# Two softmax tiles in flight and scores on 64x32 array tiles: one change to a fused AdaLN, attention, GRU and FFN kernel

## The chip, the cores and the metric

The kernel runs on one core of a Trainium2 chip. The metric is the device time in microseconds (us) of one execution, lower is better. Five engines matter: TensorE (PE for its matmuls, PEld for its weight loads), VectorE (DVE), ScalarE (ACT), GpSimd (POOL) and SyncE (SP), which issues all the DMAs. Each runs its own list of instructions in order and waits for the others on semaphores.

## The reference, cut to what matters

```python
# x [128, 32, 256]; cond [128, 256]; 32 heads of 8
x = x + attention(cond_adaln(x, query=cond[1]))      # part A
x = x + ffn(gru(initial_state=cond, inputs=x))       # part B

def cond_adaln(x):     # 8 block sums per sequence, softmax-weighted, projected, added; layer norm
    blk  = x.reshape(B, 8, 4, 256).sum(2)
    keys = rms_norm(blk @ Wk.T) * rms_weight
    w    = softmax(keys @ query)
    return layer_norm(x + (w @ blk) @ Wo.T) * gamma + beta

def attention(h):      # causal, with a linear position bias
    q, k, v = split(h @ W_attn + b_attn)
    s = q @ k.T / sqrt(8)                            # per head, 32 x 32
    p = softmax(where(causal, s, -10000) + bias)
    return (p @ v) @ W_proj + b_proj

def gru(h, xs):        # 32 sequential steps on [128, 256]
    r, z = sigmoid(...), sigmoid(...)
    n = tanh(x @ Wn + bn + r * (h @ Un + cn))
    h = (1 - z) * n + z * h
```

## The kernel before, in words

Part A takes the first 320 us of the profile, part B the rest; the change touches part A. The 4096 tokens are 8 groups (`NG`) of 4 tiles; a tile is 128 tokens, which are 4 sequences (`TB`) of 32 tokens. Group g, tile i of it, is tile n = 4g + i. Everything is float32; a float32 matmul stands in the trace as two pairs of weight load and matmul, a transpose as one.

Work per tile, with the lines that do it:

- Scores (PE, L1090): 8 matmuls of 128x128x128 (16 records). They need the keys and the queries laid out so that one matmul makes 4 heads for all 4 sequences. `qbd` and `kbd` are zero outside of their blocks. To fill them, queries and keys are written from SBUF to DRAM (`save_qk`, L308) and read back in the other layout (`load_q`, L314, 4 DMAs for half a group; `load_k`, L323, 4 DMAs for half a group).
- Mask (DVE, L766), maximum (DVE, L774), subtraction (DVE, L778), each in two halves of 128x512; exponential (ACT, L535).
- Transposes of the probabilities (PE, L1102, 8), copied out of PSUM by ACT (L471, `pT`).
- Probabilities times values (PE, L1113): 32 matmuls with 32 columns of weights and 40 moving columns, each on one of four column tiles of the array (`tile_position=(0, 32*b)`), 64 records.
- Reciprocal and normalisation (DVE, L785 and L789), transposes (PE, L1123), copy (ACT, `oT`), output projection (PE, L1131), residual (DVE, L801).

Work per group, spread over the four steps of the group before it or of the one before that: block sums (DVE, L671), their products with the weights (PE, L995, into `ps_a`), a chain of short steps for the block weights (`cond_sums`, `cond_scores`, `cond_row`, `cond_shift`, `cond_exp`, `cond_normalise`, `cond_col`, `select_blocks`), `spread_proj` (PE, L1019), `add_proj` with its statistics (DVE, L728, L733), `mean_and_variance` (DVE, L741), `inverse_std` (POOL), `normalise_tokens` (ACT, L490), `transpose_y` (PE, L1033) with its copies (ACT, L498), and the projections of q and k (PE, L1044) and of v (PE, L1053).

The order is written out by hand, for each engine in a function `tile_step`. Before, PE does in step n: scores of tile n + 1; probabilities-times-values of tile n; its transposes and output projection; and the transposes of the probabilities of tile n + 1. So tile n is finished in its own step. The group's extras stand between them: q in step i = 0, k in 1, v and `spread_proj` in 2, and the block products of group g + 3 in step 3, for which DVE does `block_sums(g + 3)` two steps earlier, in step 1:

```python
                if cond_ahead and i == 1:
                    block_sums(g + 3, l_xf, DMA * (g + 1))
```

Five of the groups run in a loop of the engines' sequencers (`Fori`), the last three are written out.

Of the kernel before, what the change touches and what calls it, by code (L numbers as in the profile page):

```python
# [10 lines left out]
F32 = mybir.dt.float32  # L11
# [7 lines left out]
P = 128  # L19
# [4 lines left out]
NG = B // GB  # L24
HG = 4
NQ = NH // HG
# [45 lines left out]
def adaln_attn_gru_ffn(nc, x_tok, x_feat, cond_t, wkwo, wqkv, wp, wih, whh, wf, vecs, rows, consts, q_dram, k_dram,  # L72
                       v_dram, out):
    ctx = ExitStack()
    with ctx:
# [53 lines left out]
        with ExitStack() as attention_only:  # L129
            qbd = attention_only.enter_context(nc.sbuf_tensor("qbd", [P, GH, NQ, TB, HT], F32))  # L130
            kbd = attention_only.enter_context(nc.sbuf_tensor("kbd", [P, HG, GH, NQ, HT], F32))
            vbd = attention_only.enter_context(nc.sbuf_tensor("vbd", [P, HG + 1, GH, TB, TH * VW], F32))
            qn = attention_only.enter_context(nc.sbuf_tensor("qn", [P, C, GH * TB, HT], F32))
            kn = attention_only.enter_context(nc.sbuf_tensor("kn", [P, C, GH * TB, HT], F32))
# [73 lines left out]
        q_saved = sem("q_saved")  # L208
        k_saved = sem("k_saved")
# [10 lines left out]
        q_in = [sem("q_in0"), sem("q_in1")]  # L220
# [67 lines left out]
        def _(sp):  # L288
# [14 lines left out]
            sp.wait_ge(zeroed, 4)  # L303


            def save_qk(dram, src, k, saved, chunks=range(C)):
                for m in chunks:
                    sp.dma_start(dram[bass.ds(k, 1), :, m * P:(m + 1) * P, :].rearrange("o x p n -> p (o x) n"),  # L308
                                 src[:, m, :, :]).then_inc(saved, DMA)

            def load_q(k, half):

                for b in range(TB):
                    sp.dma_start(qbd[32 * b:32 * b + 32, half, :, b, :],  # L314
                                 q_dram[bass.ds(k, 1), half * TB + b, :, :].rearrange(
                                     "o (r q) n -> (o r) q n", q=NQ)).then_inc(q_in[half], DMA)

            def load_k(k, half):

                for j in range(HG):  # L320
                    rows = k_dram[bass.ds(k, 1), half * TB:(half + 1) * TB, :, :].rearrange(
                        "o b (d j q) n -> (o b d) j (q n)", j=HG, q=NQ)
                    sp.dma_start(kbd[j:P:HG, j, half, :, :].rearrange("p q n -> p (q n)"),  # L323
                                 rows[:, j, :]).then_inc(k_in[half], DMA)
# [16 lines left out]
            sp.wait_ge(q_out, C)  # L341
            save_qk(q_dram, qn, 0, q_saved)
            for m in range(C):
                sp.wait_ge(k_out, m + 1)
                save_qk(k_dram, kn, 0, k_saved, (m,))
            sp.wait_ge(q_saved, C * DMA)
            load_q(0, 0)
            sp.wait_ge(k_saved, C * DMA)
            load_k(0, 0)
            sp.wait_ge(v_out, 2)  # L350
# [4 lines left out]
            load_q(0, 1)  # L355
            load_k(0, 1)
            load_v(0, 1)

            def group_loads(g, norm_ahead, cond_ahead):
# [22 lines left out]
                load_q(g + 1, 1)  # L382
# [11 lines left out]
            with sp.Fori(0, NG - 3) as g:  # L394
                group_loads(g, True, True)
# [26 lines left out]
        def _(pool):  # L422
# [4 lines left out]
            nc.gpsimd.memset(qbd[:, :, :, :, :], 0.0).then_inc(zeroed, 1)  # L427
            nc.gpsimd.memset(kbd[:, :, :, :, :], 0.0).then_inc(zeroed, 1)
# [40 lines left out]
        def _(act):  # L469
# [32 lines left out]
            def feature_out(k, m, dst, order, done, out_sem, saved, bias, scale):  # L502

                act.wait_ge(done, C * k + m + 1)
                if m == 0:
                    act.wait_ge(saved, C * DMA * k)
                for half in range(GH):
                    src = ps_a[:, m * GC + half * TH * P:m * GC + (half + 1) * TH * P]
                    last = nc.scalar.activation(
                        dst[:, m, half * TB:(half + 1) * TB, :].rearrange(f"p b {order} -> p b t s", t=TH),  # L510
                        src.rearrange("p (t b s) -> p b t s", t=TH, b=TB), ACT.Identity,
                        bias=bias[:, m:m + 1], scale=scale)
                last.then_inc(out_sem, 1)

            def q_chunk(k, m):

                feature_out(k, m, qn, "(s t)", q_mm, q_out, q_saved, bq, SCALE)

            def k_chunk(k, m):
                feature_out(k, m, kn, "(t s)", k_mm, k_out, k_saved, vec[:, V_BK:V_BK + C], 1.0)  # L520
# [48 lines left out]
            probs_out(0)  # L569

            def tile_step(g, i, norm_ahead, cond_ahead):

                n = GT * g + i
                if i == 0:
                    transpose_out(g + 1)
                if i == 3:
                    if norm_ahead:
                        normalise_tokens(g + 2, (0, 1))
                    attn_out(n)
                    if norm_ahead:  # L580
                        normalise_tokens(g + 2, (2, 3))
                if i == 2:
                    v_half(g + 1, 0)
                    v_half(g + 1, 1)
                softmax_exp(n + 1, (i + 1) % 2)
                if cond_ahead and i == 3:
                    cond_out(g + 3, ps_a[:, 0:512])
                if i == 0:
                    q_chunk(g + 1, 0)
                if i == 1:  # L590
                    k_chunk(g + 1, 0)
                if i < 3:
                    attn_out(n)
                if norm_ahead and i == 1:
                    cond_exp(g + 2)
                if i == 0:
                    q_chunk(g + 1, 1)
                if i == 1:
                    k_chunk(g + 1, 1)
                probs_out(n + 1)  # L600

            with act.Fori(0, NG - 3) as g:
                for i in range(GT):
                    tile_step(g, i, True, True)
            for i in range(GT):
                tile_step(NG - 3, i, True, False)
            act.wait_ge(wqkv_lo, 3)
            act.wait_ge(w_ready, 2)
            for i in range(GT):
                tile_step(NG - 2, i, False, False)  # L610

                if i < C:
                    copy_out(w_ih_r[0][:, i, :], w_ih[:, i, :]).then_inc(w_hi, 1)
                elif i == C:
                    copy_out(w_f_r[0][:, :, :], w_f[:, :, :]).then_inc(w_hi, 1)
# [764 lines left out]
```

## Time and profile before

| what | value |
|---|---|
| runs | 505.97, 506.21, 507.70 us, median 506.21 |
| the profiled execution | 506.46 us, of which the span of the trace is 504.4 |
| TensorE clock, mean of the span | 0.988 of full speed |
| part A ends (last residual) | 319.7 us |
| one group of part A in the loop | 34.3 us |

The span is the time from the first to the last instruction that the profiler sees; what the execution took beyond it, 2.1 us, is not split up. PE's busy share is a union of records that overlap, and the end of a matmul is modelled, so a busy PE may still be waiting for a tenth of a microsecond here and there. The spacing of starts in a run of equal instructions is the better measure of what one costs.

### The profile page before, as it was taken

The numbers are of one execution on the slowest core, as the hardware profiler recorded it, in microseconds if no ns is written. First come the engines' busy times: TensorE is split into PE (matmuls) and PEld (weight loads), VectorE is DVE, ScalarE is ACT, GpSimd is POOL, SyncE is SP. The second block draws the span as 40 slices with busy tenths as digits, with TensorE's granted clock in tenths as the row PEclk, the third lists the DMA queues.
The fourth block names the chain that finished last, engine by engine and source line by source line (L and its number), as shares of the span: only waits on it lengthen the run. The fifth ranks groups of instructions, "written<-read, shape, count | busy, mean of one in ns | idle before, by whom it ended". The sixth has DMA issues, their size and how long they took to land.

```text
span 504.4 us, 13154 instructions
## 1 busy us (share of the span) xinstructions
PE 468.7 (93%) x4962; PEld 406.6 (81%) x4962; DVE 359.6 (71%) x1049; ACT 242.1 (48%) x584; POOL 49.6 (10%) x67
## 2 busy tenths in 40 slices
PE   7489899999999999999989978799999999999995
PEld 5258688797888897988878867788999999999994
DVE  3814689698797897896877688456767677676675
ACT  1252554836557547457465625344444444444341
POOL 7321201201202112012012000000000000000000
PEclk9969999999999999999999999999999999999999
DMA  8515443454433444433432330000001010010101
GB/s 304 206 51 156 133 125 97 132 129 118 146 98 110 141 107 150 122 93 114 108 107 67 99 106 6 3 0 2 21 22 43 2 42 22 21 44 1 42 22 64
DMA packets 81863, 42.59 MB, mean 84 GB/s; under 512 B 53793, under 2 KB 74913, under 8 KB 81825
## 3 DMA queue, kind: packets, MB, share of 16 engines
q1 hardware_dynamic: 81824, 42.07, 28.3%
q8 instruction: 25, 0.41, 0.4%
q14 instruction: 14, 0.11, 0.1%
HBM read 25.28 MB, written 16.78 MB: 83 GB/s over the span
## 4 chain that ended last, share of the span: by engine, by line
PE 65%; DVE 11%; ACT 6%; issue 5%; POOL 3%; DMA 2%; SPq 2%; POOLq 0%; DVEq 0%; ACTq 0%
PE ps_s L1090 6%; PE ps_s L1257 6%; PE ps_t L1257 6%; PE ps_o L1257 5%; PE ps_t L1102 5%; PE ps_s L1229 5%; PE ps_a L1044 4%; PE ps_t L1229 4%; PE ps_a L1053 4%; PE ps_m L1131 4%; PE ps_a L1229 4%; PE ps_m L1229 3%; POOL yT_r L452 3%; PE ps_a L1019 3%; DVE mx L774 3%
## 5 line engine op out<-in xcount | busy, mean ns | idle before, releaser
L1090 PE MATMUL ps_s<-kbd,qbd 128*128 128x128 f32 x512 | 65.7, 282 | 0.0
L535 ACT ACTIVATE sc<-sc 128x512 f32<-128x512 f32 x64 | 38.8, 628 | 54.4 <-DVE sc L778 54.4
L766 DVE COPY_PREDICATED masked<-kst,ps_s 128x512 f32<-128x512 int32 x64 | 46.8, 741 | 24.1 <-issue 20.0
L1090 PEld LDWEIGHTS ps_s<-kbd,qbd 128*128 128x128 f32 x512 | 62.9, 196 | 0.1
L1044 PE MATMUL ps_a<-yT_r,w_qkv_r 128*128 128x512 f32 x192 | 53.3, 422 | 2.6 <-ACT yT_r L498 1.5
L1044 PEld LDWEIGHTS ps_a<-yT_r,w_qkv_r 128*128 128x128 f32 x192 | 35.7, 196 | 14.4 <-POOL yT_r L452 4.9
L778 DVE TENSOR_TENSOR sc<-masked,mx 128x512 f32<-128x512 f32 x64 | 41.0, 680 | 0.0
L774 DVE TENSOR_REDUCE mx<-masked 128x16 f32<-128x512 f32 x64 | 40.4, 671 | 0.0
L1102 PE MATMUL ps_t<-kst,sc 128*128 128x128 f32 x256 | 35.2, 277 | 4.6 <-ACT sc L535 4.6
L631 ACT ACTIVATE zg<-ps_t,brz 128x128 f32<-128x128 f32 x64 | 20.0, 364 | 38.8 <-PE ps_t L1257 38.8
L911 DVE SCALAR_TENSOR_TENSOR rg<-ps_o,vec,rg 128x128 f32<-128x128 f32 x64 | 19.5, 346 | 26.8 <-PE ps_o L1257 22.9
L801 DVE SCALAR_TENSOR_TENSOR xf<-ps_m,b_out,xf 128x128 f32 (+1 forms) x64 | 24.8, 434 | 19.0 <-PE ps_m L1131 19.0
L1257 PEld LDWEIGHTS ps_s<-hT,w_hh 128*128 128x128 f32 x256 | 33.1, 191 | 4.5 <-DVE hT L929 2.4
L1131 PE MATMUL ps_m<-oT,w_p 128*128 128x128 f32 x256 | 34.1, 276 | 1.4 <-ACT oT L471 1.4
L1102 PEld LDWEIGHTS ps_t<-kst,sc 128*128 128x128 f32 x256 | 28.3, 141 | 8.7 <-ACT sc L535 8.7
L471 ACT ACTIVATE pT<-ps_t 128x512 f32<-128x512 f32 x64 | 34.9, 597 | 0.8
L1131 PEld LDWEIGHTS ps_m<-oT,w_p 128*128 128x128 f32 x256 | 31.5, 192 | 4.5 <-ACT oT L471 4.3
L1257 PE MATMUL ps_s<-hT,w_hh 128*128 128x128 f32 x256 | 34.2, 276 | 0.9 <-DVE hT L929 0.6
L1257 PE MATMUL ps_o<-hT,w_hh 128*128 128x128 f32 x256 | 33.8, 275 | 0.0
L1257 PE MATMUL ps_t<-hT,w_hh 128*128 128x128 f32 x256 | 33.8, 275 | 0.0
L631 ACT ACTIVATE rg<-ps_s,brz 128x128 f32<-128x128 f32 x64 | 20.0, 363 | 23.7 <-PE ps_s L1257 23.7
L1257 PEld LDWEIGHTS ps_t<-hT,w_hh 128*128 128x128 f32 x256 | 31.2, 192 | 0.1
(108 smaller groups left out, 844.7 us busy)
## 6 DMA issues: line engine op xcount, KB each, us to landing
xf<-in_x_feat SPq DMA_DIRECT2D x8, 512.0 KB, 4.0
xg<-in_x_tok SPq DMA_DIRECT2D x8, 512.0 KB, 4.5
q_dram<-qn SPq DMA_DIRECT2D x16, 256.0 KB, 3.1
k_dram<-kn SPq DMA_DIRECT2D x16, 256.0 KB, 2.9
qbd<-q_dram SPq DMA_DIRECT2D x64, 64.0 KB, 2.4
kbd<-k_dram SPq DMA_DIRECT2D x64, 64.0 KB, 2.2
v_dram<-vn SPq DMA_DIRECT2D x16, 256.0 KB, 2.5
vbd<-v_dram SPq DMA_DIRECT2D x64, 64.0 KB, 2.0
```

What stands on the lines that cost most here:

```text
L471: return nc.scalar.activation(dst, src, ACT.Copy)
L535: nc.scalar.activation(part, part, ACT.Exp).then_inc(sc_exp, 1)
L631: nc.scalar.activation(dst[:, c, :], gate_part(gate, c, t), ACT.Sigmoid, bias=brz[:, b0 + c:b0 + c + 1]).then_inc(done, 1)
L766: nc.vector.copy_predicated(kept, keep.unsqueeze(1).to_broadcast([P, NH // 2, S]), ps_s[:, h * 512:(h + 1) * 512].rearrange("p (h k) -> p ...
L774: nc.vector.tensor_reduce(m, kept, axis=AX_X, op=ALU.max).then_inc(sc_max, 1)
L778: nc.vector.tensor_tensor(shifted, kept, m.unsqueeze(2).to_broadcast([P, NH // 2, S]), ALU.subtract).then_inc(sc_sub, 1)
L1044: last = nc.tensor.matmul(bank, w_qkv_r[a][:, c, first_col + m * P:first_col + (m + 1) * P], yT_r[b][:, c, :], start=(a == b == c == 0), s ...
L1090: last = nc.tensor.matmul(bank[:, q * P:(q + 1) * P], tile_q[:, i % TH, :], kbd[:, :, i // TH, h * HW + q, cols], start=True, stop=True)
L1102: last = nc.tensor.transpose(ps_t[:, col:col + P], sc[:, p, col:col + P], ident)
L1131: last = nc.tensor.matmul(ps_m[:, E + m * P:E + (m + 1) * P], w_p[:, c, m * P:(m + 1) * P], oT[:, c, :], start=(c == 0), stop=(c == C - 1))
L1229: last = nc.tensor.matmul(dst, w_r[a][:, c, col:col + P], rhs_r[b][:, c, :], start=first, stop=(c == C - 1 and a == 1), skip_group_check=True)
L1257: last = nc.tensor.matmul(dst, w_hh[:, c, col + m * P:col + (m + 1) * P], old[:, c, :], start=(which is None and c == 0 and m == 0), stop= ...
```

## The change

Four things change together.

1. Scores on 64x32 tiles of the array. Queries stay where ACT writes them (`qn`, now two buffers of [128, 2, 512]) and serve as weights of 64 rows and 32 columns, one sequence each. Keys are spread over `kbd`, [128, 2, 8, 512], zero but for partitions p with p mod 8 = h in slot h. A tile's scores are 16 matmuls (32 records) of 256 moving columns, on eight positions: two halves of the rows (r) times four column tiles (b). Row half 0 writes the first PSUM bank of `ps_s`, row half 1 the second.
2. Keys reach `kbd` by one DMA hop inside SBUF, 8 DMAs of 32 KB for half a group, after both k chunks are out. `q_dram`, `k_dram`, `qbd`, `save_qk` and `load_q` go.
3. A new order with two tiles in flight. Attention output of tile n - 1 (transposes, projection, normalisation, residual) moves into step n, beside the scores of tile n + 1 and the transposes of probabilities and the product with the values of tile n.
4. The group's extras move: `block_sums(g + 3)` from step 1 to the end of DVE's step 3; `spread_proj` from step 2 to step 1, and `add_proj` to the end of DVE's step 1; both halves of q, k and v stand together. The `Fori` loops of SP, ACT, DVE and PE are written out.

```diff
@@ scores, PE
-                pe.wait_ge(k_in[i // 2], HG * DMA * (g + 1))
-                pe.wait_ge(q_in[i // 2], TB * DMA * (g + 1))
-                for h in range(2):
-                    if not first:
-                        pe.wait_ge(sc_out, 2 * n - 1 + h)
-                    bank = ps_s[:, h * 512:(h + 1) * 512]
-                    for q in range(HW):
...
+                pe.wait_ge(k_in[i // 2], KH * DMA * (g + 1))
+                pe.wait_ge(q_out, C * (g + 1))
+                if not first:
+                    pe.wait_ge(sc_out, 2 * n)
+                for c in range(C):
+                    for r in range(RH):
+                        rows = slice(r * P // RH, (r + 1) * P // RH)
+                        for b in range(TB):
+                            cols = slice(i * P + b * S, i * P + (b + 1) * S)
+                            out_cols = slice((r * C + c) * KH * S, (r * C + c + 1) * KH * S)
+                            last = nc.tensor.matmul(ps_s[b * S:(b + 1) * S, out_cols], qn[rows, g % 2, c, cols],
+                                                    kbd[rows, c, :, cols], start=True, stop=True,
+                                                    tile_position=(r * P // RH, b * S))
+                        if c == C - 1:
+                            last.then_inc(sc_mm, 1)
@@ load_k, SP
+                cols = slice(half * TH * P, (half + 1) * TH * P)
+                for h in range(KH):
+                    sp.dma_start(kbd[h:P:KH, :, h, cols], kn[h:P:KH, :, cols]).then_inc(k_in[half], DMA)
@@ tile_step, PE, after the change
+                if i == 0 and not last_group:
+                    transpose_y(g + 1, norm_ahead)
+                if n + 1 < NT:
+                    scores(n + 1, (n + 1) // GT, (n + 1) % GT)
+                if n > 0:
+                    transpose_attn(n - 1)
+                transpose_probs(n, n % 2, first=(n == 0))
+                if n > 0:
+                    project_out(n - 1)
+                if norm_ahead and i == 1:
+                    cond_col(g + 2)
+                if i < 3 and not last_group:
+                    work_ahead(g + 1, i, 0)
+                    work_ahead(g + 1, i, 1)
+                if norm_ahead and i == 0:
+                    cond_row(g + 2)
+                if g + 3 < NG and i == 3:
+                    pe.wait_ge(v_out, 2 * g + 4)
+                    block_products(g + 3, ps_a[:, 0:512])
+                if norm_ahead and i == 1:
+                    pe.wait_ge(ra_ready, g + 3)
+                probs_v(n, g, i)
+                if norm_ahead and i == 1:
+                    pe.wait_ge(k_out, 2 * g + 4)
+                    spread_proj(g + 2)
@@ tile_step, DVE, after the change
+                if n > 0:
+                    normalise(n - 1)
+                if norm_ahead and i == 1:
+                    cond_shift(g + 2)
+                if n + 1 < NT:
+                    softmax_mask(n + 1, (n + 1) % 2)
...
+                if n + 1 < NT:
+                    softmax_max(n + 1, (n + 1) % 2)
...
+                if n + 1 < NT:
+                    softmax_shift(n + 1, (n + 1) % 2)
...
+                if n > 0:
+                    residual(n - 1, (n - 1) // GT, (n - 1) % GT)
+                if norm_ahead and i == 1:
+                    add_proj(g + 2)
+                if g + 3 < NG and i == 3:
+                    block_sums(g + 3, l_xf, DMA * (g + 1))
@@ ACT: tile_step's order becomes attn_out(n - 1), probs_out(n), copies of q, k or v,
@@ normalise_tokens (i == 3), softmax_exp(n + 1), cond_out(g + 3) (i == 3)
@@ SP, group_loads
-                sp.wait_ge(q_out, 2 * g + 4)
-                save_qk(q_dram, qn, g + 1, q_saved)
+                sp.wait_ge(k_out, 2 * g + 4)
                 sp.wait_ge(sc_mm, 8 * g + 4)
-                sp.wait_ge(q_saved, C * DMA * g + 2 * C * DMA)
-                load_q(g + 1, 0)
-                sp.wait_ge(k_out, 2 * g + 3)
-                save_qk(k_dram, kn, g + 1, k_saved, (0,))
-                sp.wait_ge(k_out, 2 * g + 4)
-                save_qk(k_dram, kn, g + 1, k_saved, (1,))
-                sp.wait_ge(k_saved, C * DMA * g + 2 * C * DMA)
                 load_k(g + 1, 0)
                 sp.wait_ge(sc_mm, 8 * g + 8)
                 load_k(g + 1, 1)
-                load_q(g + 1, 1)
```

## Rows read from the trace of the kernel before

**Rows 1.** The page: busy times, granted clock in 40 slices, chain by engine.
```profile
PE 468.7 (93%) x4962; PEld 406.6 (81%) x4962; DVE 359.6 (71%) x1049; ACT 242.1 (48%) x584; POOL 49.6 (10%) x67
PEclk9969999999999999999999999999999999999999
PE 65%; DVE 11%; ACT 6%; issue 5%; POOL 3%; DMA 2%; SPq 2%; POOLq 0%; DVEq 0%; ACTq 0%
```

**Rows 2.** Busy time by stretch: a looped group, the last three; length stands second.
```profile
core 0: us, PE busy (x) PEld busy (x) DVE busy (x) ACT busy (x) POOL busy (x), PEclk, DMA share, GB/s
153.86:188.21 34.35, 33.85 (x467) 28.98 (x466) 28.50 (x75) 19.75 (x40) 4.67 (x8) 1.00 0.44 123
...
229.47:264.05 34.58, 32.23 (x462) 28.31 (x461) 26.77 (x71) 19.45 (x41) 4.66 (x7) 1.00 0.40 108
264.05:296.08 32.03, 28.80 (x443) 25.43 (x441) 23.49 (x51) 18.41 (x36) 2.58 (x2) 1.00 0.32 84
296.08:319.70 23.62, 18.52 (x379) 16.59 (x376) 17.19 (x41) 9.25 (x19) 0.00 (x0) 1.00 0.12 36
```

**Rows 3.** Timeline, TensorE: start, length, line, operation, tiles, records; idle time ahead in brackets.
```profile
149.80 1.03 PE L1019 MATMUL ps_a<-kw_sb,ra 128*128 128x256 f32 x4
150.77 0.90 PEld L1102 LDWEIGHTS ps_t<-kst,sc 128*128 128x128 f32 x8
151.65 0.97 PEld L1131 LDWEIGHTS ps_m<-oT,w_p 128*128 128x128 f32 x8
152.65 2.05 PE L1090 MATMUL ps_s<-kbd,qbd 128*128 128x128 f32 x16
154.62 0.68 PEld L1113 LDWEIGHTS ps_o<-vbd,pT 128*32 128x32 f32 x64
155.36 1.12 PE L995 MATMUL ps_a<-w_kwo,blkT 128*128 128x512 f32 x2
156.34 0.20 PEld L1123 LDWEIGHTS ps_m<-kst,on 128*128 128x128 f32 x2 [0.69 <-DVE on L789]
160.07 0.87 PEld L1033 LDWEIGHTS ps_a<-kst,y 128*128 128x128 f32 x8 [0.24 <-issue]
171.94 2.60 PEld L1044 LDWEIGHTS ps_a<-yT_r,w_qkv_r 128*128 128x128 f32 x12
179.36 2.82 PEld L1053 LDWEIGHTS ps_a<-w_qkv_r,yT_r 128*128 128x128 f32 x24
```

**Rows 4.** Timeline, VectorE, from the same group.
```profile
151.47 1.40 DVE L733 BATCH_NORM_STATS2 st<-y 128x6 f32<-128x256 f32 x4
155.47 0.36 DVE L785 RECIPROCAL rden<-ps_o 128x32 f32<-128x32 f32 x1
156.21 1.27 DVE L774 TENSOR_REDUCE mx<-masked 128x16 f32<-128x512 f32 x2
157.39 1.28 DVE L778 TENSOR_TENSOR sc<-masked,mx 128x512 f32<-128x512 f32 x2
158.68 0.79 DVE L801 SCALAR_TENSOR_TENSOR xf<-ps_m,b_out,xf 128x128 f32 x2
175.49 1.98 DVE L671 TENSOR_REDUCE blkT<-xf 128x128 f32 x2
178.84 0.71 DVE L766 COPY_PREDICATED masked<-kst,ps_s 128x512 f32<-128x512 int32 x1
179.47 0.72 DVE L766 COPY_PREDICATED masked<-kst,ps_s 128x512 f32<-128x512 int32 x1
```

**Rows 5.** Timeline, the issue of eight DMAs by SP; page, their landing.
```profile
179.78 5.25 SPq L323 DMA_DIRECT2D kbd<-k_dram  x8
...
kbd<-k_dram SPq DMA_DIRECT2D x64, 64.0 KB, 2.2
```

**Rows 6.** Busy time and granted clock around a pause of TensorE at the start.
```profile
20.70:24.90 4.20, 0.00 (x0) 0.00 (x0) 4.03 (x19) 1.01 (x2) 2.59 (x4) 1.00 0.00 0
24.91:35.15 10.24, 8.43 (x20) 5.12 (x20) 0.16 (x1) 5.29 (x10) 3.07 (x3) 0.50 0.16 51
```

More of the change, by code:

```diff
@@ L24 @@
 NG = B // GB
+NT = B // TB
 HG = 4
+RH = 2
+KH = P // RH // 8
 NQ = NH // HG
@@ L69, with adaln_attn_gru_ffn @@
 NCONST = K_SPREAD + GC
-def adaln_attn_gru_ffn(nc, x_tok, x_feat, cond_t, wkwo, wqkv, wp, wih, whh, wf, vecs, rows, consts, q_dram, k_dram,
-                       v_dram, out):
+def adaln_attn_gru_ffn(nc, x_tok, x_feat, cond_t, wkwo, wqkv, wp, wih, whh, wf, vecs, rows, consts, v_dram, out):
     ctx = ExitStack()
@@ L301, in _ @@
             sp.dma_start(hT[:, 1, :, :], cond_t).then_inc(l_gru, DMA)
[L303 to L316, printed above, removed]
-            def load_k(k, half):
[L320 to L324, printed above, removed]
+            sp.wait_ge(zeroed, 3)
+            def load_k(k, half):
+                cols = slice(half * TH * P, (half + 1) * TH * P)
+                for h in range(KH):
+                    sp.dma_start(kbd[h:P:KH, :, h, cols], kn[h:P:KH, :, cols]).then_inc(k_in[half], DMA)
             def save_v(k, half):
@@ L340, in _ @@
             sp.dma_start(xg[:, :, :], x_group(1)).then_inc(l_xg, DMA)
[L341 to L348, printed above, removed]
+            sp.wait_ge(k_out, C)
             load_k(0, 0)
+            load_k(0, 1)
             sp.wait_ge(v_out, 2)
@@ L392, in group_loads @@
                 load_v(g + 1, 1)
-            with sp.Fori(0, NG - 3) as g:
+            for g in range(NG - 3):
                 group_loads(g, True, True)
@@ L500, in transpose_out @@
                                              scale=vec[:, V_GAMMA + c:V_GAMMA + c + 1]).then_inc(out_sem, 1)
[L502 to L513, printed above, removed]
-            def q_chunk(k, m):
-                feature_out(k, m, qn, "(s t)", q_mm, q_out, q_saved, bq, SCALE)
-            def k_chunk(k, m):
-                feature_out(k, m, kn, "(t s)", k_mm, k_out, k_saved, vec[:, V_BK:V_BK + C], 1.0)
+            def q_chunk(k, m):
+                act.wait_ge(q_mm, C * k + m + 1)
+                if m == 0 and k >= 2:
+                    act.wait_ge(sc_mm, 2 * GT * (k - 1))
+                nc.scalar.activation(qn[:, k % 2, m, :], ps_a[:, m * GC:(m + 1) * GC], ACT.Identity,
+                                     bias=bq[:, m:m + 1], scale=SCALE).then_inc(q_out, 1)
+            def k_chunk(k, m):
+                act.wait_ge(k_mm, C * k + m + 1)
+                if m == 0 and k >= 1:
+                    for half in range(GH):
+                        act.wait_ge(k_in[half], KH * DMA * k)
+                nc.scalar.activation(kn[:, m, :], ps_a[:, m * GC:(m + 1) * GC], ACT.Identity,
+                                     bias=vec[:, V_BK + m:V_BK + m + 1], scale=1.0).then_inc(k_out, 1)
             def v_half(k, half):
@@ new lines, in tile_step @@
+                if g == NG - 2 and i <= C:
+                    if i == 0:
+                        act.wait_ge(wqkv_lo, 3)
+                        act.wait_ge(w_ready, 2)
+                    if i < C:
+                        copy_out(w_ih_r[0][:, i, :], w_ih[:, i, :]).then_inc(w_hi, 1)
+                    else:
+                        copy_out(w_f_r[0][:, :, :], w_f[:, :, :]).then_inc(w_hi, 1)
+            for g in range(NG):
+                for i in range(GT):
+                    tile_step(g, i)
@@ L1170, in _, with tile_step @@
             block_products(2, ps_a[:, 0:512])
-            transpose_probs(0, 0, first=True)
-            def tile_step(g, i, norm_ahead, cond_ahead):
+            def tile_step(g, i):
                 n = GT * g + i
-                if i == 0:
+                last_group, norm_ahead = g + 1 == NG, g + 2 < NG
+                if i == 0 and not last_group:
                     transpose_y(g + 1, norm_ahead)
-                scores(n + 1, g + (i + 1) // GT, (i + 1) % GT)
+                if n + 1 < NT:
+                    scores(n + 1, (n + 1) // GT, (n + 1) % GT)
+                if n > 0:
+                    transpose_attn(n - 1)
+                transpose_probs(n, n % 2, first=(n == 0))
+                if n > 0:
+                    project_out(n - 1)
```

182 lines of the change are left out of this document (47 added, 135 removed).

## The prediction, made before the changed kernel was run
> **What bounds the kernel now.** I read the page first for the busy shares and the clock. PE is busy 93% of the span, DVE 71%, ACT 48%, the chain that ended last is 65% PE, and the granted clock is full in nearly every slice [rows 1]. Part A is what the change touches, so next come the stretches: a looped group takes 34.35 us, of which PE is busy 33.85 and DVE 28.50 [rows 2]. Busy overlaps pauses, so I priced PE by the spacing of starts in the timeline, (length of the run - one record) / (records - 1). Scores: (2.05 - 0.28)/15 = 0.118 us a record, 1.88 a tile. In the same way a tile's transposes of probabilities take 0.87, its output projection 0.94, its two small transposes 0.22 and probabilities-times-values 0.58 [rows 3]. Per group: spread_proj 8 x 0.215 = 1.72 (spacing (1.03 - 0.38)/3, where 0.38 is a record's modelled length), block products with twice the columns 4 x 0.43 = 1.72, transposes of y 0.87, q and k 2.58 each, v 2.76, the small matmuls of the block weights 0.4 [rows 3]. The sum is 4 x 4.49 + 12.6 = 30.6 us, and with 0.1 for each of eight changes between a full-array matmul and the column tiles, 31.4. So 3 us of a group is waiting, and PE sets the pace.
>
> DVE in the same units: mask 2 x 0.63 = 1.26 (starts 178.84 and 179.47), maximum 1.18 (156.21 to 157.39), subtraction 1.19, reciprocal and normalisation 0.74, residual 0.70, which is 5.07 a tile; statistics 1.44, block sums 1.91, the add of the projection 1.25, and about 3 for the short steps [rows 4]. Together 20.3 + 7.6 = 27.9 us a group, 3.5 less than PE. This second bound matters: if PE got cheaper by more, DVE would stop it.
>
> **The change, part by part.**
>
> *Scores.* 16 matmuls of 256 moving columns are 32 records. One record with 256 float32 columns takes 0.215 us (L1019) [rows 3]. What counts is how many run at once. For the four column tiles there is a row: L1113 has 64 records in (0.68 - 0.11)/63 = 0.009 us each, where a full-array record of 128 columns takes 0.118; 40 columns in proportion would be 0.037, so four run at once [rows 3]. No row shows two row halves at once. Bounds: all eight at once, 4 x 0.215 = 0.86 us; row halves one after the other, 8 x 0.215 = 1.73; nothing at once, 32 x 0.215 = 6.9, which the row of L1113 makes improbable; no gain below 0.86 is possible, since each tile's own columns must stream. If starts keep program order but both halves overlap otherwise, it is 5 x 0.215 = 1.08. I take 1.08: the halves have different rows and different banks, as the column tiles have different partitions. So 1.88 becomes 1.08 plus 0.2 for two more changes of array tiling per tile: 0.6 saved, 2.4 a group. The 0.1 is from the trace: the last score record starts at 152.65 + 2.05 - 0.28 = 154.42, and the first of L1113 at 154.62, 0.20 later instead of 0.118 [rows 3].
>
> The Trainium skill, page "TensorEngine Tiling (Array Packing)", section "Gotcha 1: PSUM Pressure", says that different row tiles can't use the same PSUM bank at the same time. The code gives each half its own bank, so by this rule the sum stays; no row here shows whether that is all it takes, and if the halves did exclude each other, the sum would be that of the second rival below.
>
> *DMA.* q's two hops and k's first hop go. The new load_k has 8 issues for half a group; 8 took 5.25 us before, landing 2.2 [rows 5], so keys are there 7.4 us after k is out. K comes out late in step 1 and its first reader is the scores in step 3, 9 us later: hidden with about 2 us to spare. What is behind it on SP (save and load of v) has two steps. Smaller pieces may take from 0.4 to 0.9 us to issue; at 0.9 the keys are late by about 1 us a group, 6 in all. I take 0. ACT writes q and k in one piece instead of two; ACT is at 48% [rows 1], no gain. Writing out the loops: the written-out group 6 took 34.58 against 34.35 for a looped one [rows 2], so nothing for it, at most 0.5 a group.
>
> *Order.* I walked the lists of PE, DVE and ACT: an instruction starts when its engine is free and its waits are met, with the durations above. The old order walked this way gives 33.9 a group against 34.35 measured, 0.45 short, which I leave in both. The new order, from the start of one score block to the next:
> - Step 0: scores with their change 1.18, small transposes 0.22, transposes of probabilities 0.87, wait 0.53 (ACT is at its four copies of y), output projection 0.94, q 2.58, row 0.2, values 0.78, change 0.1: 7.4.
> - Step 1: 1.18 + 0.22 + 0.87 + 0.94, wait 0.32 for the block weights, 0.2, k 2.58, values 0.78, spread_proj 1.72, change 0.1: 8.9.
> - Step 2: 1.18, wait 0.45 (normalise stands behind add_proj on DVE), 0.22 + 0.87 + 0.94, v 2.76, 0.78, 0.1: 7.3.
> - Step 3 is where the order hurts. PE is through scores, transposes and projection at 1.18 + 0.22 + 0.87 + 0.94 = 3.2 and then wants the block products of group g + 3. DVE makes their sums last in its step 3: normalise, mask, maximum, subtraction, residual, then the sums, 0.3 + 0.74 + 1.26 + 1.18 + 1.19 + 0.70 + 1.91 = 7.3, with semaphores 7.4. PE waits 4.2 us. Queued behind that wait on PE are the products (1.72), the values of tile n (0.78), the transposes of y (0.87) and the next scores; DVE waits for the values, 2.8 us, then 1.0 for the scores. 7.4 + 1.72 + 0.78 + 0.87 + 0.2 = 11.0.
>
> Sum 34.6 against 33.9: a looped group gets 0.7 longer although PE has 2.4 less to do. DVE's side says the same: 27.9 of work + 2.8 + 1.0 + 1.25 + 1.55 (before the normalisation of step 1 and for spread_proj) = 34.5. Four groups go this way, the first +0.1. The sixth has no sums ahead, its step 3 is 6.4: 30.0 against 33.8, -3.8. The seventh, without the block weights: 7.6 + 6.8 + 7.4 + 4.2 = 26.0 against 32.0, -6.0 (the row has 32.03, with PE busy for 28.80 [rows 2]). The last tiles and the last output part, which now is a step later: +1.6; the first tile -0.4. Total: 0.1 + 2.8 - 3.8 - 6.0 + 1.6 - 0.4 = -5.7. The prologue keeps its length (ahead of the first scores PE has 12 warm-up products, and the keys' way has become shorter), part B doesn't change. The profiled execution took 506.46, its span 504.4; 506.46 - 5.7 = 500.8, and 0.25 more than the median is within the runs' spread. I say 501.
>
> **The rivals.**
>
> *Clock.* In the trace PE did nothing from 20.70 to 24.90, 4.2 us, at full clock, and then the granted clock was 0.50 (1.2 GHz) for 10.24 us [rows 6]. The wait forecast for step 3 is as long, five times. For: equal length. Against: a similar pause need not always do it, and the pause may come out at 3.8. Price: during a fall everything on PE takes double, so a fall as long as the row's costs 5.1 us where the chain is PE's, and one of half that length 2.6. With two or three of five falling, some +7: 508; with all five for 10 us, 526. The Trainium skill, page "TensorE: Matmul & The Clock Gate", section "Why this matters for your kernels", asks for no idle gaps between bursts of matmuls; the old part A has none like it, and by that rule the new order loses in each group, which is this rival.
>
> *Row halves one after the other.* Scores 1.73: steps 2 and 3 become PE's, walked 35.6 a group, 31.3 and 27.3 at the end: +2.4 in all, 509. This is the side on which the change is slower; it decides from about 1.55 us a tile. For: no row shows two halves. Against: other rows, other bank.
>
> *The DVE bound alone.* If the wait of step 3 is filled (the sums earlier than I think), a group is DVE's 27.9 plus some 3 of waits, 31: 5 x -3.6 more, 483. Against: sums are written last.
>
> *The change doesn't do it.* DMA issue at 0.9 us, or semaphores eat the rest: 506.
>
> **How the numbers follow.** Forecast 0.43; clock 0.21; halves in series 0.19; DVE bound 0.07; no effect 0.06; pairs of passes that block each other, 3.46 us a tile, some 560, 0.04. The likeliest alone spans 496 to 505. For 8 in 10 it must take in 508 and 509 and some falls of the clock, and below it 492: 492 to 515. What can be told from no change here is 0.5%, 2.5 us. Faster: 0.43 x 0.85 + 0.21 x 0.2 + 0.19 x 0.1 + 0.07 + 0.06 x 0.2 = 0.51. Same: 0.06 + 0.07 + 0.06 + 0.04 = 0.23. Slower: 0.26.
>
> **What would show it.** In the profile after: L671 behind the residual, and PE's wait for blkT at the block products, about 4 us, five times; scores of 32 records in about 1.1 us of starts, where 0.86 or 1.73 tells the halves; score blocks 11.0, 7.4, 8.9, 7.3 apart; groups of 34.6 to 35 in the loop part, 30 and 26 after it. The granted clock below 1.0 in part A would show the second case. The forecast is wrong if PE doesn't wait at the block products, if the keys are late at step 3 (a wait for kbd), or if the scores take over 1.5 us.

## The result, and the profile after

The changed kernel takes 518.4 us (median of four runs, 516.86 to 519.89), the kernel before 506.09 beside it: ratio 1.0239, 95% interval 1.02 to 1.0278. It is slower, by 2.0 to 2.8%, and lies above the predicted range. The profiled execution took 518.16 us against 506.46, so there are 11.7 us to explain, and 17.4 from the forecast of -5.7. All of it lies in part A: from the start of the first score matmul to that of the last residual it was 268.8 us before (50.42 to 319.26), and is 280.7 after (50.12 to 330.83). The kernel before took 506.09, 506.97, 507.39 and 506.55 us in four sets of runs (this one, then experiments 1 to 4, 5 to 8 and 9 to 12), so times of different sets compare to about 1 us; the ratios are taken within a set.

The page of the changed kernel: busy times, clock in 40 slices, the chain by engine, then the two groups of PE that the change is about (line, engine, operation, tiles, count | busy us, mean ns | idle time ahead, what ended it) and the landing of the keys.
```profile
PE 450.4 (87%) x5474; PEld 367.6 (71%) x5474; DVE 361.4 (70%) x1049; ACT 238.7 (46%) x552; POOL 50.4 (10%) x66
...
PEclk9969999899899899998999989899999999999999
...
PE 64%; DVE 19%; issue 7%; ACT 4%; SPq 3%; DMA 2%; POOL 1%; DVEq 0%; ACTq 0%; POOLq 0%
...
L942 PE MATMUL ps_a<-w_kwo,blkT 128*128 128x512 f32 x28 | 20.4, 868 | 22.1 <-DVE blkT L617 21.8
...
L1040 PE MATMUL ps_s<-kbd,qn 64*32 64x256 f32 x1024 | 35.4, 382 | 0.7 <-DMA kbd<-kn 0.7
...
kbd<-kn SPq DMA_DIRECT2D x128, 32.0 KB, 1.9
```
PE has 18 us less to do than before [rows 1] and the span is longer. The block products (L942) wait 21.8 us for DVE's sums, and the clock line has an 8 at nearly regular distances, where before it was all 9 behind the start [rows 1].

Busy time by stretch of the changed kernel: a looped group, and the last two groups of work ahead.
```profile
134.10:171.67 37.57, 31.66 (x537) 23.87 (x540) 28.90 (x73) 19.35 (x37) 4.82 (x7) 0.95 0.24 72
247.00:277.51 30.51, 28.59 (x533) 22.63 (x536) 26.47 (x70) 18.15 (x35) 4.81 (x7) 1.00 0.19 54
277.51:303.58 26.07, 24.41 (x513) 19.82 (x517) 20.86 (x47) 17.34 (x32) 2.55 (x2) 1.00 0.18 51
```
The answering rows of before are 34.35, 34.58 and 32.03 [rows 2]. The groups without block sums got shorter by 4 and 6 us; each looped group got longer by 3.2, with 0.95 as mean clock.

Timeline of the end of step 3 in such a group, TensorE and then VectorE, and the window of the clock in it (length, busy times, granted clock as in [rows 2]).
```profile
198.61 1.06 PE L1082 MATMUL ps_m<-oT,w_p 128*128 128x128 f32 x8
203.97 3.15 PE L942 MATMUL ps_a<-w_kwo,blkT 128*128 128x512 f32 x4 [4.30 <-DVE blkT L617]
207.06 1.19 PE L1064 MATMUL ps_o<-vbd,pT 128*32 128x40 f32 x64
208.18 1.09 PE L980 MATMUL ps_a<-kst,y 128*128 128x128 f32 x8
```
```profile
198.86 1.25 DVE L723 TENSOR_REDUCE mx<-masked 128x16 f32<-128x512 f32 x2
200.03 1.28 DVE L729 TENSOR_TENSOR sc<-masked,mx 128x512 f32<-128x512 f32 x2
201.23 0.77 DVE L752 SCALAR_TENSOR_TENSOR xf<-ps_m,b_out,xf 128x128 f32<-128x128 f32 x2
201.91 1.92 DVE L617 TENSOR_REDUCE blkT<-xf 128x128 f32<-128x512 f32 x2
...
208.33 0.36 DVE L736 RECIPROCAL rden<-ps_o 128x32 f32<-128x32 f32 x1 [4.50 <-PE ps_o L1064]
```
```profile
170.51:204.64 34.13, 28.21 (x477) 22.45 (x467) 28.95 (x73) 18.76 (x35) 4.82 (x7) 1.00 0.26 79
204.64:208.05 3.41, 3.41 (x67) 1.39 (x66) 0.00 (x0) 0.60 (x1) 0.00 (x0) 0.51 0.02 5
```
PE stands from 199.67 to 203.97 while DVE goes through maximum, subtraction, residual and sums. Right behind, from 204.6, the granted clock is 0.5 (1.2 GHz) for 3.41 us: the block products take 3.15 us where a group at full clock has 1.98 (below), values 1.19 instead of 0.80, and DVE waits for just these values. Four falls begin at 129.5, 167.0, 204.6 and 242.1, 37.5 us apart, the length of a group; one ahead of them, at 88.5, lasts 6.83 us. Two more of 3.41 lie in the tail.

### The profile page after: what moved, and what is told of

Read it like the earlier page. It is cut to its first block, busy times and chain, and to the rows that moved or that the text cites. A ratio compares the mean times of both kernels' runs of the same rounds, so it can differ in the third digit from the quotient of the medians.

```text
span 516.0 us, 13519 instructions
## 1 busy us (share of the span) xinstructions
PE 450.4 (87%) x5474; PEld 367.6 (71%) x5474; DVE 361.4 (70%) x1049; ACT 238.7 (46%) x552; POOL 50.4 (10%) x66
## 4 chain that ended last, share of the span: by engine, by line
PE 64%; DVE 19%; issue 7%; ACT 4%; SPq 3%; DMA 2%; POOL 1%; DVEq 0%; ACTq 0%; POOLq 0%
PE ps_a L991 6%; PE ps_s L1191 6%; PE ps_t L1191 6%; PE ps_o L1191 5%; PE ps_s L1163 5%; PE ps_t L1163 4%; PE ps_a L942 4%; PE ps_a L1000 4%; PE ps_a L1163 4%; PE ps_s L1040 3%; PE ps_o L1064 3%; PE ps_m L1163 3%; DVE mx L723 3%; PE ps_a L966 3%; DVE sc L729 3%
## 5 line engine op out<-in xcount | busy, mean ns | idle before, releaser
L991 PE MATMUL ps_a<-yT_r,w_qkv_r 128*128 128x512 f32 x192 | 50.8, 414 | 2.5 <-ACT yT_r L463 1.5
L715 DVE COPY_PREDICATED masked<-kst,ps_s 128x512 f32<-128x512 int32 x64 | 43.9, 735 | 4.5 <-issue 3.8
L497 ACT ACTIVATE sc<-sc 128x512 f32<-128x512 f32 x64 | 36.9, 620 | 7.1 <-DVE sc L729 7.1
L1082 PE MATMUL ps_m<-oT,w_p 128*128 128x128 f32 x256 | 36.5, 288 | 3.7 <-ACT oT L436 3.7
L942 PE MATMUL ps_a<-w_kwo,blkT 128*128 128x512 f32 x28 | 20.4, 868 | 22.1 <-DVE blkT L617 21.8
L1082 PEld LDWEIGHTS ps_m<-oT,w_p 128*128 128x128 f32 x256 | 32.7, 200 | 5.4 <-ACT oT L436 5.3
L1040 PE MATMUL ps_s<-kbd,qn 64*32 64x256 f32 x1024 | 35.4, 382 | 0.7 <-DMA kbd<-kn 0.7
L1191 PE MATMUL ps_s<-hT,w_hh 128*128 128x128 f32 x256 | 34.2, 276 | 0.9 <-DVE hT L876 0.6
L1053 PE MATMUL ps_t<-kst,sc 128*128 128x128 f32 x256 | 34.2, 278 | 0.0
L1064 PEld LDWEIGHTS ps_o<-vbd,pT 128*32 128x32 f32 x2048 | 24.9, 120 | 12.8 <-issue 10.6
L1191 PE MATMUL ps_o<-hT,w_hh 128*128 128x128 f32 x256 | 33.8, 275 | 0.0
L1191 PE MATMUL ps_t<-hT,w_hh 128*128 128x128 f32 x256 | 33.8, 275 | 0.0
L736 DVE RECIPROCAL rden<-ps_o 128x32 f32<-128x32 f32 x32 | 11.4, 356 | 29.5 <-PE ps_o L1064 29.5
L1191 PEld LDWEIGHTS ps_o<-hT,w_hh 128*128 128x128 f32 x256 | 31.2, 192 | 0.0
```

Source lines behind the costliest of these rows:

```text
L497: nc.scalar.activation(part, part, ACT.Exp).then_inc(sc_exp, 1)
L715: nc.vector.copy_predicated(kept, keep.unsqueeze(1).to_broadcast([P, NH // 2, S]), ps_s[:, h * 512:(h + 1) * 512].rearrange("p (h k) -> p ...
L942: last = nc.tensor.matmul(bank, blkT[:, c, :, :].rearrange("p b n -> p (b n)"), w_kwo[:, c, :], start=(c == 0), stop=(c == C - 1))
L991: last = nc.tensor.matmul(bank, w_qkv_r[a][:, c, first_col + m * P:first_col + (m + 1) * P], yT_r[b][:, c, :], start=(a == b == c == 0), s ...
L1040: last = nc.tensor.matmul(ps_s[b * S:(b + 1) * S, out_cols], qn[rows, g % 2, c, cols], kbd[rows, c, :, cols], start=True, stop=True, tile_ ...
L1064: last = nc.tensor.matmul(ps_o[32 * b:32 * b + 32, q * 40:(q + 1) * 40], pT[:, q, 32 * b:32 * b + 32], vbd[:, :, i // TH, b, col:col + HD] ...
```

## The experiments

The unchanged rest in each is the named base kernel. Each time is the median of three to ten executions, and ratios are to the kernel before, with the 95% interval. Lengths of steps and groups are taken between the starts of the transposes of probabilities, where nothing else is said.

**1. The changed kernel with the pause filled.** Without a use for their result, nine products run where PE waits.
```diff
                     pe.wait_ge(v_out, 2 * g + 4)
+                    for _ in range(9):
+                        nc.tensor.matmul(ps_a[:, 512:768], oT[:, 0, :],
+                                         oT[:, :, :].rearrange("p c n -> p (c n)"),
+                                         start=True, stop=True)
                     block_products(g + 3, ps_a[:, 0:512])
```


> The changed kernel with nine 128x128x256 products (0.43 us each, 3.9 in all) put on PE in step 3 between the output projection and the wait for the block sums, into half of ps_a that is free then. The sums stay where they are, so DVE's wait for PE and the order stay; only PE isn't idle. Theory A (the pause of 4.3 us costs by the clock that falls at its end, on top of the wait): granted clock 1.00 in the groups of the loop part, each 35 to 35.7 us instead of 37.6, the whole some 506 to 508. Rival B (the excess over the forecast is in the steps themselves, the clock costs little because DVE sets the pace there): groups stay at 37 or more, 515 to 518.

Measured: 507.29 us, ratio 1.0026 (0.9999 to 1.0053). A looped group of this kernel, and PE in its step 3:
```profile
130.95:166.97 36.02, 33.99 (x548) 26.47 (x547) 28.93 (x75) 19.36 (x37) 4.82 (x7) 1.00 0.25 75
```
```profile
157.55 4.05 PE L1146 MATMUL ps_a<-oT 128*128 128x256 f32 x18
162.01 1.98 PE L942 MATMUL ps_a<-w_kwo,blkT 128*128 128x512 f32 x4 [0.41 <-DVE blkT L617]
```
PE still waits for the sums after the nine products, so nothing was made earlier by them, and more work gave 11.1 us back. The clock is full in all looped groups. Five groups took 190.0 us in the changed kernel and 180.6 here: 9.4 of the 11 come from there, 3.2 from the first group (fall of 6.83 us) and 1.55 from each other (fall of 3.41).

**2. The sums a step earlier.** The changed kernel with one number different: `if g + 3 < NG and i == 3` becomes `i == 2` at DVE's `block_sums`.

> The changed kernel with block_sums(g + 3) at the end of DVE's step 2 instead of step 3. Theory A: PE's 4.3 us wait at the block products goes, and with it the fall of the clock; but DVE has the same 27.9 us of work a group, so that a group is 33.6 to 34.5, not 31: 500 to 504. Rival B (the wait only moves, to the scores or transposes of step 3, long enough that the clock still falls): groups of 36 and more, 512. Rival C (PE bound, all of the wait is gained): 31 a group, 487.

Measured: 499.53 us, ratio 0.9859 (0.9833 to 0.9886). Groups take 34.2 us at full clock:
```profile
135.47:169.67 34.20, 29.86 (x530) 23.13 (x529) 28.84 (x74) 19.24 (x36) 4.81 (x7) 1.00 0.26 79
```
So the place of one DVE operation carries 18.9 us: 11 of clock, the rest the wait itself.

**3. The new scores alone.** The kernel before, its loops written out, with the 64x32 scores and the keys' hop; order as before.

> The kernel before with the scores on eight tiles and the keys by one hop alone; the order of the kernel before stays, its loops written out. Theory A (the scores are a gain of 0.6 to 0.7 us a tile and the order is what costs): groups of 33.2 to 33.5 instead of 34.35, 498 to 500 in all, clock 1.00. Rival B (the new scores don't help, since the mask of both halves now waits for the end of the scores or the keys come late): 505 to 508.

Measured: 499.41 us, ratio 0.9866 (0.9836 to 0.9897).
```profile
129.36:162.32 32.96, 30.51 (x531) 23.50 (x529) 27.98 (x76) 19.50 (x37) 4.65 (x7) 1.00 0.26 80
```

**4. The new order alone.** The changed kernel with the old scores and the keys and queries through DRAM.

> The changed kernel with the scores, qbd, kbd and the way by DRAM of the kernel before; the new order stays. Theory A: PE still waits for the block sums in step 3, about 3.5 us, groups of 36.6 without a fall of the clock and 38 to 39 with one: 523 to 530, slower than the whole change. Rival B (the order is not what costs): 505 to 510.

Measured: 528.13 us, ratio 1.0423 (1.0394 to 1.0451). A looped group, and the waits of PE (us in total, times, longest):
```profile
146.52:185.44 38.92, 34.29 (x466) 29.50 (x465) 29.25 (x73) 20.25 (x40) 4.64 (x7) 0.96 0.40 110
```
```profile
PE ps_a L983 <- DVE blkT L658: 20.0, 6, 3.9
```
The same wait, a fall of the clock in every looped group, and no cheaper scores to pay for it.

**5. The loops written out, nothing else.** `with pe.Fori(0, NG - 3) as g` becomes `for g in range(NG - 3)`, likewise on ACT, DVE and SP.

> The kernel before with its four Fori loops of five rounds written out, nothing else: the instructions on the engines are the same, without the loops' register work, and 0.3 MB more of instructions are fetched. Theory A (the loops cost and save nothing): 505.5 to 507.5, groups of 34.3 to 34.6. Rival B (fetching the longer lists slows PE or DVE): groups of 34.8 and more, 509. If B holds, e3's gain is larger than it looked and part of the changed kernel's loss is this.

Measured: 505.52 us, ratio 0.9974 (0.9957 to 0.9991): 0.1 to 0.4% less, of no weight beside the rest. It is the base against which experiments 3 (-6.1 us) and 4 (+22.6 us) are read. Their sum, +16.5, is more than the whole change has (+12.9): the scores are worth 6.1 in the old order and 9.7 in the new one.

**6. Experiment 2, and the sums over the condition keys behind the maximum.** On DVE, `cond_sums(g + 2)` moves from ahead of `softmax_max` to behind it in step 0.

> e2 (block sums in step 2) with cond_sums of step 0 behind the maximum instead of ahead of it. In the changed kernel and in e2 its second instruction takes 1.49 us instead of the 0.42 that it took before, and ends as GpSimd's subtraction for yT_r ends. Theory A (VectorE's instruction is held up while GpSimd's large subtractions run, for 1.07 us, and moved behind them it takes 0.42): a looped group 0.5 to 1.0 shorter than e2's 34.2, 495 to 497 in all. Rival B (it is slow for another reason, and stays at 1.49; or another instruction then takes its place beside GpSimd's): 499 to 500.

Measured: 498.55 us, ratio 0.983 (0.9788 to 0.9872), between the two expectations. The reason for it was in the changed kernel's timeline, the first three rows here; the next two are from this experiment:
```profile
172.88 2.80 POOL L417 TENSOR_TENSOR yT_r<-yT,yT_r 128x512 fp32r<-128x512 f32 x2 [12.69 <-ACT yT L463]
...
174.13 0.41 DVE L629 CUSTOM_DVE_ANT_0 junk<-kw_sb 128x256 f32<-128x256 f32 x1
...
174.46 1.49 DVE L631 CUSTOM_DVE_ANT_0 junk<-kw_sb,wqr 128x256 f32<-128x256 f32 x1
```
```profile
126.73 2.61 POOL L417 TENSOR_TENSOR yT_r<-yT,yT_r 128x512 fp32r<-128x512 f32 x2 [9.34 <-ACT yT L463]
...
129.56 0.41 DVE L631 CUSTOM_DVE_ANT_0 junk<-kw_sb,wqr 128x256 f32<-128x256 f32 x1
```
DVE's reduction takes 1.49 us beside GpSimd's subtractions and 0.41 behind them. It also took 0.42 in experiment 7 below, where it stands ahead of them. The Trainium skill, page "GPSIMD Engine Reference", section "1. Specifications", says that the two engines share their SBUF interfaces, with contention when a VectorE instruction has two SBUF inputs. This one has two, and the trace agrees. Step 0 went from 7.97 to 7.56 us and the group to 33.8.

**7. Experiment 2, and the scores ahead of the transposes of y** in PE's step 0.

> e2 with scores(n + 1) ahead of transpose_y in step 0 on PE. In e2 VectorE waits 2.3 us there for the scores, behind the transposes of y, which wait 1.0 us themselves for ScalarE's copy. Theory A (VectorE sets the pace of the new order, so what shortens its wait shortens the group): a looped group is 1.5 to 2.2 us shorter, 32.0 to 32.7, 490 to 492 in all. Rival B (PE sets the pace: its list has the same work, and the transposes of y, the copies and q only come 1.2 us later): 34, 499.

Measured: 498.55 us, ratio 0.9839 (0.9784 to 0.9895), the rival's value. Step 3 fell from 7.59 to 6.50, step 0 rose from 7.97 to 8.74: the group is 33.88, so most of the wait only moved. The reduction of experiment 6 fell to 0.42 us here too, since GpSimd's subtractions now come later; how much of the 0.3 us a group is due to that was not separated.

**8. Experiments 2, 6 and 7 together, and `add_proj` from the end of DVE's step 1 to step 2 behind the normalisation.**

> e2, e6 and e7 together, and add_proj moved from the end of VectorE's step 1 to step 2 behind the normalisation, so that the wait for spread_proj (1.9 us) is partly filled. VectorE's work is 28.5 us a group by its busy time in the trace of before; if it sets the pace, the group comes down to 30.5 to 31.5: 484 to 488 in all. Rival (PE's list is the bound by then: 23.2 of other work, 4 x 1.3 of scores, changes of tiling 0.8, and waits): no lower than 32, 490.

Measured: 498.59 us (median of 497.07, 498.59 and 502.04; a fourth execution took 504.63), ratio 0.9809 (0.9779 to 0.984). The first expectation missed by more than 10 us, the second by 8.6. The group stays at 33.7 us where the clock is full: step 1 fell from 10.13 to 9.58, step 2 rose from 8.53 to 8.9. The estimate behind "484 to 488" had added savings that lie on one ring of waits: PE waits for DVE's normalisation, which waits for PE's values. That this ring alone is why is argued, not shown: the reduction that experiment 6 had freed takes 1.48 us again in every group of this kernel but the first.

**9. Experiment 6, and the values' DMAs ahead of the second eight key DMAs** on SP (both saves of v, the load of its first half, then `load_k(g + 1, 1)`).

> The kernel with the block sums in step 2 and the condition sums behind the maximum (498.6 us), and on SP both saves of v and the load of its first half put ahead of the second eight key DMAs. There PE waits once 2.7 us for vbd in the last groups, and the granted clock falls behind that wait for 3.41 us. Theory A (the values are late because SP issues twelve key DMAs of 0.7 us first): wait and fall go, -2.7 and about -1.5: 494 to 496, no fall near 292 us. Rival B (another wait takes the place: keys of the second half now late, or the normalisation of the tile): 498 to 499.

Measured: 498.23 us, ratio 0.9848 (0.9825 to 0.9871): the rival. PE's waits in the last groups, from 240 us on, of this kernel:
```profile
PE ps_s L1040 <- DMA kbd<-kn: 3.2, 2, 2.8
```
The wait for values (2.7 us) is gone and one of 2.8 us for the keys stands in its place, with the clock fall behind it at 291.0.

**10. Experiments 6, 7 and 9 together.**

> As the one before, and on PE the scores of tile n + 1 ahead of the transposes of y in step 0. Groups measured so far with each alone: 33.8 and 33.9 us. Theory A (the two gains come from different steps and add): groups 33.4, with the values in time 492 to 494. Rival B (both shorten the same wait of PE for DVE's normalisation): groups stay 33.8, 494 to 496, the same as the one before.

Measured: 499.82 us, ratio 0.9862 (0.9832 to 0.9892). The group is 33.88 us, as with 6 or 7 alone: the gains do not add (rival B). What PE waits for is in its timeline of step 3:
```profile
184.17 1.09 PE L1040 MATMUL ps_s<-kbd,qn 64*32 64x256 f32 x32
187.10 0.44 PE L1074 MATMUL ps_m<-kst,on 128*128 128x128 f32 x2 [1.84 <-DVE on L740]
```
On DVE the normalisation stands behind the block sums, now in step 2. A second reason is in the busy times of one group, here and in experiment 6 (DVE's is the third):
```profile
134.80:168.68 33.88, 29.60 (x530) 23.19 (x529) 29.60 (x74) 19.25 (x36) 5.06 (x7) 1.00 0.26 80
126.72:160.54 33.82, 29.77 (x530) 23.15 (x529) 27.84 (x75) 19.26 (x37) 5.03 (x7) 1.00 0.26 80
```
The reduction took 0.42 us in 7 already, so 6 had nothing left to give, and put behind the maximum it now stands beside the subtractions again: 1.48 us in every group but the first, 1.07 of the 1.8 that DVE is busy longer. Experiment 7 with the values first, and this reduction left in its place, was not run. The time is also 4 us over that rival's own range; the clock, 0.974 in the mean, falls at 56.7, 84.0, 292.2 and 305.9, but the share of that was not measured.

**11. Experiment 3 with the values first**, the same edit as in 9.

> The kernel before with its loops written out and the new scores (499.4 us, groups 33.0 us), and SP's v ahead of the second keys. PE waits 2.1 us for vbd at 248.1 us there, and the clock falls for 3.41 us behind it. Theory A: -2.1 and up to -1.5, 496 to 497.5. Rival B (the normalisation or the exponential is next, as it is the cause of 9.2 and 2.7 us of waits there): 499. If A, this is faster than both kernels by 2%.

Measured: 498.55 us, ratio 0.985 (0.9826 to 0.9873). Rival B; here too PE waits once for keys, 2.1 us, where it had waited for values in experiment 3 (at 290.2, not at 248.1 as the expectation has it). The clock falls at 252.9 and 304.1. The first of these was in experiment 3 too, at 252.3, behind a wait of 1.5 us for the normalisation, which this edit doesn't touch.

**12. The old order, new scores, and only the sums late.** From experiment 3; one tile in flight.
```diff
@@ tile_step, DVE
-                if cond_ahead and i == 1:
-                    block_sums(g + 3, l_xf, DMA * (g + 1))
...
+                if cond_ahead and i == 3:
+                    block_sums(g + 3, l_xf, DMA * (g + 1))
                 residual(n, g, i)
```


> The kernel before with its loops written out and the new scores, one tile in flight, and only DVE's block sums of group g + 3 moved: from step 1 into step 3, behind the subtraction and the normalisation. PE then wants their products about 2.0 us after its scores start and DVE has the sums at 1.2 + 1.26 + 0.74 + 2.37 + 1.91 = 7.5. Theory A (the place of the sums is the cause, whatever the order of the tiles, and such a wait is followed by a fall of the clock): PE waits about 5 us five times, step 3 gets some 3.7 longer, a fall in each looped group adds 1.5 to 2: groups 38 to 38.5, 523 to 527. Rival B (the falls need the two tiles in flight): groups 36.7, clock full, 516 to 519. Rival C (the old order has the slack): under 505.

Measured: 534.12 us, ratio 1.0535 (1.0513 to 1.0556), 34.7 us more than experiment 3. A looped group, and within it the stretch of the low clock; below it PE's wait:
```profile
97.53:137.71 40.18, 32.50 (x531) 25.02 (x530) 28.41 (x73) 19.27 (x36) 4.63 (x7) 0.92 0.21 63
131.55:138.38 6.83, 6.18 (x17) 4.04 (x18) 0.76 (x2) 2.88 (x6) 0.00 (x0) 0.50 0.44 115
```
```profile
132.20 2.04 PE L959 MATMUL ps_a<-w_kwo,blkT 128*128 128x512 f32 x2 [5.85 <-DVE blkT L635]
```
Theory A in kind, and above its numbers: PE waits 5.85 us, each looped group has a fall of 6.83 us (not the half as long one that I had priced), and groups are 39.5 to 41.6. The late sums need no second tile in flight to do the damage.

## Why the prediction was wrong

What it had right:

- *Scores, eight at once.* 1.88 was to become 1.08 a tile plus 0.2 for the changes of tiling. Around a score block of the changed kernel (transposes of y, scores, small transposes):
```profile
170.76 0.93 PE L980 MATMUL ps_a<-kst,y 128*128 128x128 f32 x7
171.62 1.09 PE L1040 MATMUL ps_s<-kbd,qn 64*32 64x256 f32 x32
172.64 0.44 PE L1074 MATMUL ps_m<-kst,on 128*128 128x128 f32 x2
```
  The starts of the first and the last of the 32 records are 0.72 us apart: eight start 6.7 ns apart, and the four sets 0.22 to 0.24. The next full-array record starts 0.31 behind the last, and the change into the block adds 0.09. Together a tile costs 1.12 in the units in which I had 1.28, so the scores came a little cheaper than charged. Rival "row halves one after the other" is out.
- *The wait in step 3.* Forecast 4.2 us, five times, for `blkT`; measured 4.3 to 4.4, five times, the sums last on DVE, and DVE then waits 4.5 us for the values. With the pause filled (experiment 1) step 3 is 11.25 us long, forecast 11.0.
- *The last two groups.* 30.0 and 26.0 forecast, 30.51 and 26.07 measured. Keys cost 0.7 us once, 0.73 us to issue each (16 in 11.69). Writing out the loops costs nothing (experiment 5).

What failed is the choice at one step: the sum priced the pause of step 3 at its own length and left what follows it to a rival, "Clock", with 0.21. Its argument against was that "a similar pause need not always do it". The row for it was there, a pause of 4.20 us and then half clock [rows 6], and the forecast pause was as long. It did it in every looped group, and so did each of the five waits of 3.9 us in experiment 4 and of 5.8 us in experiment 12. (The pause of 3.1 us at the entry of part A, 56 us, had a fall behind it in one of the five kernels that have it, experiment 6.) The falls were shorter than those I had priced (10.24 us, or half of that): one of 3.41 us cost 1.55, one of 6.83 cost 3.2, a little under half their length. The Trainium skill, page "TensorE: Matmul & The Clock Gate", section "Why this matters for your kernels", warned of idle gaps between bursts of matmuls, and the traces agree for gaps of 3.9 us and more. Shorter ones go either way: 3.1 us above, 1.8 us in the last section. But with five falls at the measured price that rival comes to 501 + 9.4 = 510, not 518. So a second term was mis-sized.

The 17.4 us between forecast and measurement, by stretch of the two traces (starts of the transposes of probabilities, then the last residual; the four stretches add up to 17.5):

| stretch | before | after | change | forecast |
|---|---|---|---|---|
| first scores to first transposes | 5.3 | 8.1 | +2.8 | -0.4 |
| five looped groups | 171.8 | 190.0 | +18.2 | +2.9 |
| sixth and seventh group | 67.6 | 58.7 | -8.9 | -9.8 |
| to the last residual | 24.2 | 23.9 | -0.3 | +1.6 |

- *Five groups, 15.3 over.* 9.4 is the clock (experiment 1 against the changed kernel). The other 5.9 stands in the groups at full clock: experiment 1 has 36.3 in the first, where 34.5 had been forecast, and 36.1 in each of the four others, against 35.1. By steps of such a group, from score block to score block, it has 7.97, 9.58, 7.18 and 11.29, where the walk had 7.4, 8.9, 7.3 and 11.0 and was known to be 0.45 short. In step 0, 0.41 is DVE's reduction held up by GpSimd (experiment 6). Before, it took 0.42 us: the new order put it beside POOL's subtractions, and I had taken its duration from the trace of before without asking what would now run next to it. In step 1, 0.38 is the projection of k, which had been priced at 2.58 beside the row of its weight loads [rows 3]. Its matmuls start 0.23 us apart and the first two 0.34, and from the first of them to the first of the values it is 2.96. (q has the same price, and so had the walk of the old order, where k took 3.09 to the next record.) The 0.41 is shown by a run; the 0.38 is read from the timeline, and the rest of the 5.9 is not split up.
- *The start, 3.2 over.* The transposes of y now stand ahead of the second scores and of the first tile's transposes in PE's list, and PE waited 3.09 us there. The walk had the loop, not its entry.
- *The end.* The last groups gained 0.9 less and the tail lost 1.9 less than forecast, together -9.2 against -8.2. (Between score blocks these groups are 30.51 and 26.07; between transposes, as in the table, the later ones end 2 us later.)

The rival "DVE bound alone", 483 if the wait of step 3 were filled, fell too: with the sums earlier a group is 34.2, not 31, and no reordering that I tried brought it under 33.6. DVE is busy 27.8 to 29.6 us of these, PE 29.6 to 29.9, so neither alone is the bound; what PE waits for most is the normalisation (17.8 us, 15 times in experiment 9). With the old order and the new scores a group is 33.0 (experiment 3), shorter than any of these; the two-tile order makes that up in the last groups. Whether some order of the two-tile scheme gets down to 31 stays open.

So the change is three parts: loops written out, -0.6 to -1.9 (by the set of runs that it is compared with); cheaper scores, -6.1 in the old order; and an order that with the sums in its step 2 is worth nothing (499.53 against 499.41 without it), and with the sums in its step 3 costs 19.0. The best kernels measured are experiments 9, 6, 7, 11 and 8, 498.2 to 498.6, and 3, 2 and 10 within 1.6 us of them; their intervals overlap, so no order among them is shown, and all are faster than both kernels of the case, by 1.3 to 1.9% against the kernel before.

## What to carry to other kernels

A wait of TensorE that a trace already shows followed by half clock is to be priced with that fall in the likeliest case, every time it recurs: the wait, plus half the length of the fall (here a little less). The cheapest cure is to put the producer a step earlier, in another engine's list; filling the wait with idle products gives back the clock but not the wait. When an order is rewritten, check for each moved instruction what now runs beside it and how the loop is entered, and do not add up savings that all shorten one ring of waits.

## What the runs showed of the hardware

- A pause of 1.7 to 1.9 us on PE, for the normalisation, recurred in each looped group of experiments 2, 6, 7, 9 and 10. Behind it the clock fell for 3.41 us in two of the five groups of experiment 6 and in one of experiments 7 and 10; in experiments 2 and 9 in none. PE in the fourth group of experiment 6:
```profile
186.56 0.51 PE L1074 MATMUL ps_m<-kst,on 128*128 128x128 f32 x2 [1.85 <-DVE on L740]
186.86 1.91 PE L1053 MATMUL ps_t<-kst,sc 128*128 128x128 f32 x8
```
  The transposes take 1.91 us instead of 1.04. Experiments 6, 7 and 10 scatter by 4.1 to 5.7 us between runs and experiment 2 by 0.3. The longest run of experiment 6 has the lowest mean clock (500.58 us at 0.967) and the shortest the highest (496.49 at 0.984), so the clock takes part in it; which falls make the difference was not traced.
- A change between full-array matmuls and column or 64x32 tiles adds 0.09 to 0.10 us to the spacing of starts: 0.20 instead of 0.11 from transposes into scores, 0.31 instead of 0.22 from the last scores to the next full-array record. The 0.1 of the prediction holds. From column tiles to 64x32 tiles it is 0.13 from start to start.
- Eight 64x32 tiles, four columns of the array times two halves of its rows, with a PSUM bank for each half, run at once: eight starts 6.7 ns apart, then the next eight 0.22 to 0.24 us behind the first.
